# First feed-forward of a two-layer transformer block: a down product in plain float32 or as three products of high and low parts

## The chip, the cores and the metric

The kernel runs on one core of a Trainium2 chip. The metric is the device time in microseconds (us) of one execution. The core's engines are TensorE (PE, matrix products into PSUM), VectorE (DVE), ScalarE (ACT), GpSimd (POOL) and SyncE (SP, which issues DMAs). Each runs its own list of instructions in order; semaphores order them against each other.

## The reference

1024 tokens of 256 features pass through attention, a feed-forward, a second attention and a second feed-forward, each with a layer norm ahead and a residual add behind. The change is in the first feed-forward:

```
h = silu(x @ w_gate) * (x @ w_up)          # x: (4, 256, 256), w_gate, w_up: (256, 1024)
g = h.reshape(B, S, I // 4, 4)             # of every four hidden values keep
_, idx = top_k(abs(g), 2)                  # the two that are largest by magnitude
h_sparse = (g * mask(idx)).reshape(B, S, I)
out = h_sparse @ w_down                    # w_down: (1024, 256)
x = x + out
```

## The kernel before, in words

Hidden values lie transposed: hidden features on the 128 partitions, tokens along the free dimension. The feed-forward is cut in four quarters k = 0 to 3. Quarter k holds tokens of half k // 2 (512 tokens) and hidden features of half k % 2 (512 features, as four columns j of 128). The features are laid out so that the four columns of a quarter are the four members of each group, so the 2-of-4 choice compares whole columns. With i = 4k + j the columns are numbered 0 to 15.

**Gate and up** (`pe_gate_up`, line 1000). For each column i, 12 products on TensorE: gate and up, two halves of the contraction, and for each three products of high and low parts. This is the kernel's way to near-float32 accuracy at the rate of the rounded type fp32r: a value is split into a high part (rounded to fp32r) and a low part (value minus high), and high x high, high x low and low x high are added up in PSUM. They use PSUM banks 0 to 5, so column i waits for silu and hidden product of column i - 3.

**Activation, product, choice.** ScalarE makes silu(gate) (`act_silu`, line 1157) and VectorE multiplies it with up into the hidden buffer (`dve_hidden`, line 1266). ScalarE takes magnitudes (`act_abs`, line 1217). VectorE compares them, three ops of 1024 columns a quarter with both inputs in SBUF (`dve_compare`, line 1358), counts in 16-bit arithmetic (`dve_count`, lines 1366 to 1372) and keeps or clears the values in place, two ops of 1024 columns (`dve_keep`, line 1379), which raise the semaphore `hs`.

**Down** (`pe_down`, line 1074 for the first feed-forward, line 1078 for the second; `pe_last_down0`, line 1094, for the first one's last quarter). For each of four token tiles of a quarter TensorE adds up the four columns' products with w_down into PSUM bank 6 or 7; VectorE adds the result to x (`dve_xadd`, line 1342). In the first feed-forward the operands are plain float32: hidden buffer and raw weights. Each such product is two records in the profile. In the second, three products of parts are used, with high parts from ScalarE (line 1202) and low parts from VectorE (line 1457) in the buffers `encf`, and weights split by GpSimd in `b_w`.

**Order.** It is written out by hand. TensorE (`pe_ffn0`): columns 0 to 10, down quarter 0, columns 11 to 13, down quarter 1, columns 14 and 15, four transposes of the next layer norm, down quarter 2; quarter 3 follows in the head of the second attention. VectorE (`dve_ffn0`) does for each k two compares, a hidden product, the third compare, the first count step, a hidden product, the votes, a hidden product, then residual adds, keeps, and the last hidden product. ScalarE (`act_ffn0`) has silu and magnitudes in turn: in the round of k it is silu 4k+4, 4k+5, 4k+6, magnitudes 4k+4 and 4k+5, silu 4k+7, magnitudes 4k+6 and 4k+7. GpSimd ends the first attention with `pool_drain0` (row statistics, low parts of some weights; `ln_pool`, line 325) and then waits for the layer norm of the second attention. The down weights are loaded by SP long before, into `raw_b`. In the second attention GpSimd splits weights (`split`, lines 888 and 890) and forms sums of W2 (line 1575).

Of the kernel before, what the change touches and what calls it, by code (L numbers as in the profile page):

```python
# [22 lines left out]
F32 = mybir.dt.float32  # L23
# [3 lines left out]
ALU = mybir.AluOpType  # L27
# [9 lines left out]
UNITS = 8 * PAIRS  # L37
# [69 lines left out]
def build(nc, x_in, wa, wax, wb, wdown0, w2t, consts, scales, shuffle, out):  # L107
    with ExitStack() as ctx:
        def sb(name, shape, dt=F32):
            return ctx.enter_context(nc.sbuf_tensor(name, shape, dt))  # L110

        def sem(name):
            return ctx.enter_context(nc.semaphore(name))
# [11 lines left out]
        b_w = [[sb(f"b_{part}{s}", [P, WB_FFN], F32R) for part in ("hi", "lo")] for s in range(2)]  # L125
# [4 lines left out]
        with ExitStack() as whole:  # L130
            def sb1(name, shape):
                return whole.enter_context(nc.sbuf_tensor(name, shape, F32))
# [3 lines left out]
            raw_b = sb1("raw_b", [P, 2, WB_FFN])  # L136
# [75 lines left out]
        encf = [e[:, :, :].rearrange("p h t -> p (h t)").rearrange("p (j t) -> p j t", j=4) for e in enc]  # L212
# [34 lines left out]
        at = [{n: sem(f"L{L}_{n}") for n in names} for L in range(2)]  # L247
        raw_as = [[sem(f"L{L}_raw_a{s}") for s in range(2)] for L in range(2)]
        raw_bs = [[sem(f"L{L}_raw_b{s}") for s in range(2)] for L in range(2)]
        fnames = ("whi", "w", "gate", "up", "silu", "h", "abs", "cmp", "hs", "hi", "lo", "whi2", "w2", "down", "xadd")  # L250
        ff = [{n: sem(f"F{f}_{n}") for n in fnames} for f in range(2)]
        s_late, s_late_hi, s_late_lo = (sem("late_columns_" + n) for n in ("loaded", "high", "low"))
        s_bf, s_hadmm, s_hadev = (sem(n) for n in ("butterfly", "had_product", "w2_made"))
        s_blank, s_had = sem("blank_set"), sem("hadamard_loaded")
# [24 lines left out]
        def need_pieces(eng, f, last):  # L279

            n = pieces_until(f, last)
            if f == 0 and n > POOL_PIECES:
                eng.wait_ge(ff[0]["w2"], n - POOL_PIECES)
            else:
                eng.wait_ge(ff[f]["w"], n)
# [55 lines left out]
        def ln_act(act, st, t, bk):  # L342
            i = 8 * st + t
            act.wait_ge(ln["turned"], i + 1)
            src = bank[bk][:, 0:D].rearrange("p (c t) -> p c t", c=NC)
            nc.scalar.copy(xT[0][:, :, t * P:(t + 1) * P], src).then_inc(ln["hi"], 1)
# [539 lines left out]
        def split(hi, lo, src, eng, s_hi, wait, s_lo):  # L886

            nc.gpsimd.tensor_tensor(hi, src, zero[:, 0:1].broadcast_to(list(src.shape)), ALU.add).then_inc(s_hi, 1)  # L888
            wait()
            nc.gpsimd.tensor_tensor(lo, src, hi.bitcast(F32), ALU.subtract).then_inc(s_lo, 1)  # L890
# [158 lines left out]
        def hidden(f, k, j):  # L1049

            return hid_late[k - 2][:, j, :] if f == 0 and k >= 2 else hid[:, k % 2, j, :]

        def pe_down(pe, f, k, tiles=range(4)):
            s, L = ff[f], at[f]
            t = k % 2
            for tt in tiles:
                d = 4 * k + tt
                if tt == 0:
                    if f == 0:
                        pe.wait_ge(s["hs"], 4 * k + 4)  # L1060
                        if k < 2:
                            pe.wait_ge(raw_bs[0][t], 16 * 5)
                    else:
                        pe.wait_ge(s["hi"], 4 * k + 4)
                        pe.wait_ge(s["lo"], 4 * k + 4)
                        if k < 2:
                            need_pieces(pe, f, f"b{t}")
                if d < 2:
                    pe.wait_ge(ln["lo"], 16 * f + 16)
                if d >= 2:  # L1070
                    pe.wait_ge(s["xadd"], d - 1)
                if f == 0:
                    for j in range(4):
                        mm = pe.matmul(bank[6 + d % 2][:, 0:D], hidden(0, k, j)[:, tt * P:(tt + 1) * P],  # L1074
                                       raw_b[:, t, j * D:(j + 1) * D], start=j == 0, stop=j == 3)
                else:
                    for q, (j, (l, r)) in enumerate([(j, p) for j in range(4) for p in PASSES]):
                        mm = pe.matmul(bank[6 + d % 2][:, 0:D], encf[l][:, j, tt * P:(tt + 1) * P],  # L1078
                                       b_w[t][r][:, j * D:(j + 1) * D], start=q == 0, stop=q == 11)
                mm.then_inc(s["down"], 1)  # L1080
# [71 lines left out]
        def act_silu(act, f, i):  # L1152
            s = ff[f]
            act.wait_ge(s["gate"], i + 1)
            if i >= 2:
                act.wait_ge(s["h"], i - 1)
            nc.scalar.activation(gate[:, i % 2, :], bank[2 * (i % 3)][:, :], ACT.Silu).then_inc(s["silu"], 1)  # L1157
# [46 lines left out]
        def act_hadamard(act, q):  # L1204
            act.wait_ge(s_hadmm, q + 1)
            nc.scalar.mul(w2_a[:, 2 * q:2 * q + 2, :].rearrange("p a d -> p (a d)"), bank[S_BANK + q % 2][:, :],
                          float(HID) ** -0.5).then_inc(s_hadev, 1)

        def act_abs(act, i):

            k, j = i // 4, i % 4
            act.wait_ge(ff[0]["h"], i + 1)
            if i == 0:
                act.wait_ge(at[0]["pv"], UNITS)
            elif k and j == 0:
                act.wait_ge(ff[0]["cmp"], 3 * k)
            nc.scalar.activation(mag[:, j, :], hidden(0, k, j), ACT.Abs).then_inc(ff[0]["abs"], 1)

        def act_ffn0(act):
            for i in range(4):  # L1220
                act_abs(act, i)
            for k in range(3):
                i = 4 * (k + 1)
                act_silu(act, 0, i)
                if k == 0:
                    ln_act(act, 1, 7, 7)
                act_silu(act, 0, i + 1)
                act_silu(act, 0, i + 2)
                act_abs(act, i)
                act_abs(act, i + 1)  # L1230
                if k == 2:
                    act_next_a(act)
                act_silu(act, 0, i + 3)
                act_abs(act, i + 2)
                act_abs(act, i + 3)
            for t in range(4):
                ln_act(act, 2, t, LN2_BANK[t])
# [157 lines left out]
        def act_next_a(act):  # L1395

            act.wait_ge(raw_as[1][0], 16 * A_PARTS[1])
            act.wait_ge(ff[0]["up"], 12)
            for part in range(4):
                cs = slice(part * A0, (part + 1) * A0)  # L1400
                nc.scalar.copy(a_w[0][0][:, cs], raw_a[:, 0, cs]).then_inc(at[1]["a0hi"], 1)
# [141 lines left out]
        def pool_drain0(pool):  # L1543

            for t in range(1, 8):
                if t < 4:
                    pool.wait_ge(ln["xn"], 8 + t)
                    pool_late_lo(pool, t)
                elif t in (5, 6):
                    pool.wait_ge(ln["xn"], 8 + t)  # L1550
                    pool_piece_lo(pool, 0, t - 5)
                ln_pool(pool, 1, t)
# [134 lines left out]
        @block.gpsimd  # L1687
        def _(pool):
            nc.gpsimd.memset(zero[:, :], 0.0).then_inc(s_zero, 1)
            nc.gpsimd.memset(neg_half[:, :], -0.5).then_inc(s_half, 1)  # L1690
            nc.gpsimd.memset(rms_eps[:, :], RMS_EPS).then_inc(s_half, 1)
            pool.wait_ge(s_zero, 1)
            pool.wait_ge(s_half, 2)
            for t in range(2):
                ln_pool(pool, 0, t)
            pool.wait_ge(s_rope, 16)
            pool.wait_ge(s_scl, 16)
            for a in (2, 0):
                if a == 0:
                    pool.wait_ge(s_scq, 1)  # L1700
                nc.gpsimd.tensor_tensor(cos_t[:, :, a, :], cos_c, scl[:, a // 2, :].unsqueeze(1).broadcast_to([P, 2, DH]),
                                        ALU.mult).then_inc(s_cos, 1)
            ln_pool_two(pool, 0, 2)
            pool_b(pool, 0, None, 0, 0)
            slots(pool, 0, pool_slot, pool_head0, pool_tail(pool, 0))
            pool_drain0(pool)
            for t in range(4):
                ln_pool(pool, 2, t)
            slots(pool, 1, pool_slot, pool_head, pool_tail(pool, 1))
            for n in range(2, 5):  # L1710
                pool_piece_lo(pool, 1, n)
            for n in range(5, len(pieces[1])):
                if pieces[1][n][0] == "b1" and pieces[1][n - 1][0] == "b0":
                    pool.wait_ge(ff[1]["lo"], 4)
                pool_piece(pool, 1, n)
# [4 lines left out]
        def _(act):  # L1720
# [8 lines left out]
            for L in range(2):  # L1729
# [35 lines left out]
                if L == 0:  # L1765
                    act_drain0(act)
                (act_ffn0, act_ffn1)[L](act)

        @block.vector
# [216 lines left out]
```

## Time and profile before

| | |
|---|---|
| median of 3 runs | 673.9 us (673.75 to 675.7) |
| profiled execution | 675.06 us |
| its span | 673.3 us |
| granted TensorE clock, mean | 0.997 |
| busy: PE, DVE, ACT, POOL | 98%, 83%, 66%, 53% of the span |

Busy is the share of the span in which an engine had at least one instruction at work. Products overlap in the pipe and their ends are modelled, so a product's duration (0.28 us for 256 columns) is more than the distance between two starts. Times of rows are us from the span's start.

### The profile page before, as it was taken

To read this page: it belongs to the slowest core of one execution; us is meant where nothing else is said; L and a number is where in the kernel's file an instruction comes from. 1 tells how busy PE (TensorE), PEld (TensorE's weight loads), DVE (VectorE), ACT (ScalarE), POOL (GpSimd) and SP (SyncE) were. 2 spreads that over 40 slices of the span, in tenths; PEclk is the share of its full clock that TensorE was granted. 3 is DMA by queue.
4 is the path that set the end of the run, shared out by engine and by line. 5 is a ranking of instruction groups with operands and counts; after the bars stand their busy time and mean duration, and the time that the engine had idled before them with its cause. 6 is when DMAs were issued, how large, how long until landed. Compare 5 with 4: busy or idle time off the path is not lost.

```text
span 673.3 us, 15093 instructions
## 1 busy us (share of the span) xinstructions
PE 659.8 (98%) x4153; PEld 588.3 (87%) x4153; DVE 556.0 (83%) x1705; ACT 446.8 (66%) x1721; POOL 360.1 (53%) x557
## 2 busy tenths in 40 slices
PE   8899999999999998999999999999999999999998
PEld 4689999999999997888879999999999999978887
DVE  7889999899989878969866998989999898795443
ACT  3899999999999875422347676666676666763222
POOL 5899999999999944002068961523232324028000
PEclk8999999999999999999999999999999999999999
DMA  7156666765656640100035656566556656000000
GB/s 243 38 129 137 136 144 156 169 135 133 141 125 139 130 173 0 48 1 1 16 107 121 155 124 152 116 142 135 135 132 130 142 125 139 17 1 1 1 31 32
DMA packets 242594, 69.55 MB, mean 103 GB/s; under 512 B 184400, under 2 KB 238544, under 8 KB 242384
## 3 DMA queue, kind: packets, MB, share of 16 engines
q1 hardware_dynamic: 219280, 56.53, 38.1%
q10 hardware_dynamic: 23232, 12.06, 6.0%
q8 instruction: 35, 0.57, 0.4%
q14 instruction: 47, 0.39, 0.2%
HBM read 45.29 MB, written 23.27 MB: 102 GB/s over the span
## 4 chain that ended last, share of the span: by engine, by line
PE 89%; DVE 6%; issue 2%; POOL 1%; ACT 1%; DVEq 0%; POOLq 0%; ACTq 0%
PE bank L543 13%; PE bank L427 12%; PE bank L1000 12%; PE bank L535 11%; PE bank L564 7%; PE bank L395 6%; PE bank L470 4%; PE bank L388 4%; PE bank L472 4%; PE bank L487 3%; PE bank L1074 3%; PE bank L465 3%; PE bank L1078 3%; DVE x L743 1%; PE bank L1094 1%
## 5 line engine op out<-in xcount | busy, mean ns | idle before, releaser
L713 ACT ACTIVATE probs<-scores,negmax 128x128 f32<-128x128 f32 (+1 forms) x256 | 117.1, 470 | 6.1 <-DVE negmax L798 4.9
L621 ACT CAST enc_hi<-bank 128x256 fp32r<-128x256 f32 x128 | 48.8, 381 | 66.0 <-PE bank L472 62.6
L888 POOL TENSOR_TENSOR a_hi<-raw_a,zero 128x384 fp32r<-128x384 f32 (+1 forms) x60 | 44.2, 736 | 71.1 <-PE bank L564 71.1
L325 POOL TENSOR_TENSOR ln_r<-ln_ve,neg_half 128x1 f32<-128x1 f32 x26 | 17.0, 654 | 118.3 <-DVE ln_ve L299 118.3
L427 PE MATMUL bank<-b_hi,enc_hi 128*128 128x256 f32 x256 | 77.8, 304 | 0.5 <-DVE x L743 0.5
L774 DVE STREAM_TRANSPOSE blocks<-probs 128x384 f32<-128x384 f32 x113 | 64.8, 574 | 11.7 <-ACT probs L713 9.9
L427 PE MATMUL bank<-b_hi,enc_lo 128*128 128x256 f32 x256 | 72.1, 282 | 0.0
L427 PE MATMUL bank<-b_lo,enc_hi 128*128 128x256 f32 x256 | 71.8, 281 | 0.0
L743 DVE SCALAR_TENSOR_TENSOR x<-bank,rinv,x 128x256 f32<-128x256 f32 x144 | 67.4, 468 | 2.2 <-PE bank L427 0.9
L754 DVE TENSOR_TENSOR enc_lo<-bank,enc_hi 128x256 fp32r<-128x256 f32 x128 | 53.4, 417 | 16.5 <-PE bank L395 9.4
L906 POOL TENSOR_TENSOR rot_a<-rot_a,rot_b 128x384 f32<-128x384 f32 x64 | 64.9, 1014 | 0.2 <-DVE rot_b L875 0.2
L904 POOL TENSOR_TENSOR rms_r<-meansq,neg_half 128x3 f32<-128x3 f32 x64 | 54.8, 856 | 6.6 <-DVE meansq L873 2.3
L1157 ACT ACTIVATE gate<-bank 128x512 f32<-128x512 f32 x32 | 19.1, 598 | 58.7 <-PE bank L1000 57.9
L890 POOL TENSOR_TENSOR a_lo<-raw_a,a_hi 128x384 fp32r<-128x384 f32 (+1 forms) x60 | 53.8, 896 | 4.7
L535 PE MATMUL bank<-a_hi,xT_hi 128*128 128x512 f32 x128 | 51.9, 408 | 2.7 <-DVE xT_lo L352 1.7
L713 ACT ACTIVATION_READ_ACCUMULATOR probs<-scores,negmax 128x1 f32 x256 | 53.4, 209 | 0.0
L543 PE MATMUL bank<-xT_hi,a_hi 128*128 128x512 f32 x128 | 52.0, 406 | 0.3 <-DVE xT_lo L352 0.3
L661 ACT ACTIVATE gate<-bank 128x128 f32<-128x128 f32 x192 | 50.6, 282 | 1.8 <-PE bank L535 1.8
L427 PEld LDWEIGHTS bank<-b_hi,enc_hi 128*128 128x128 f32 x256 | 48.5, 189 | 3.4 <-issue 0.9
L543 PE MATMUL bank<-xT_lo,a_hi 128*128 128x512 f32 x128 | 50.5, 395 | 0.0
L427 PEld LDWEIGHTS bank<-b_lo,enc_hi 128*128 128x128 f32 x256 | 48.5, 190 | 2.3
L543 PE MATMUL bank<-xT_hi,a_lo 128*128 128x512 f32 x128 | 50.3, 393 | 0.0
(186 smaller groups left out, 2330.6 us busy)
## 6 DMA issues: line engine op xcount, KB each, us to landing
arrived<-shuffle SPq DMA_DIRECT2D x452, 48.0 KB, 2.2
shuffle<-blocks ACTq DMA_DIRECT2D x57, 192.0 KB, 2.5
shuffle<-blocks SPq DMA_DIRECT2D x56, 192.0 KB, 2.5
raw_a<-in_wa SPq DMA_DIRECT2D x40, 192.0 KB, 3.2
raw_b<-in_wb SPq DMA_DIRECT2D x16, 256.0 KB, 3.0
raw_a<-in_wa SPq DMA_DIRECT2D x32, 128.0 KB, 2.7
hid_last<-in_wax SPq DMA_DIRECT2D x2, 512.0 KB, 3.8
w_a<-in_w2t SPq DMA_DIRECT2D x1, 1024.0 KB, 5.3
```

What stands on the lines that cost most here:

```text
L427: mm = pe.matmul(output_bank(L, m)[:, cols], enc[l][:, h, t * P:(t + 1) * P], b_w[slot][r][:, h * D:(h + 1) * D], start=i == 0 and not (on ...
L535: mm = pe.matmul(ps[:, :], xT[l][:, g, t * P:(t + 1) * P], a_w[slot][r][:, g * 512:(g + 1) * 512], start=i == 0, stop=i == 5)
L543: mm = pe.matmul(ps[:, :], a_w[slot][l][:, g * 768 + w * P:g * 768 + (w + 1) * P], xT[r][:, g, half * 512:(half + 1) * 512], start=i == 0, ...
L661: nc.scalar.activation(gate[:, m % 2, a * DH:(a + 1) * DH], bank[PJ_BANK + m % 2][:, a * DH:(a + 1) * DH], ACT.Square, scale=float(DH) ** ...
L713: nc.scalar.activation(probs[:, c % 4, c0:c1], scores[:, c % 2, c0:c1], ACT.Exp, bias=negmax[:, c % 2, r:r + 1], scale=-1.0, accum_out=row ...
L743: nc.vector.scalar_tensor_tensor(out=x[:, m % 8, :], in0=output_bank(L, m)[:, hh * D:(hh + 1) * D], scalar=rinv[:, u, r:r + 1], in1=x[:, m ...
L754: nc.vector.tensor_tensor(enc[1][:, w % 2, dst], bank[O_BANK][:, 0:D], enc[0][:, w % 2, dst].bitcast(F32), ALU.subtract).then_inc(s["elo"], 1)
L774: nc.vector.transpose(blocks[:, c % 2, :], probs[:, c % 4, :]).then_inc(s_blocks[L], 1)
L890: nc.gpsimd.tensor_tensor(lo, src, hi.bitcast(F32), ALU.subtract).then_inc(s_lo, 1)
L904: nc.gpsimd.tensor_tensor(rms_r[:, t, :], meansq[:, m % 2, :], neg_half[:, 0:3], ALU.pow).then_inc(s["rp"], 1)
L906: nc.gpsimd.tensor_tensor(rot_a[:, m % 2, :], rot_a[:, m % 2, :], rot_b[:, m % 2, :], ALU.add).then_inc(s["radd"], 1)
L1000: mm = pe.matmul(ps[:, :], a_w[t][l][:, c0:c0 + P], xT[rr][:, g, th * 512:(th + 1) * 512], start=q == 0, stop=q == 5)
```

## The change

In quarters 0 and 1 of the first feed-forward the down product becomes three products of parts, as in the second feed-forward; quarters 2 and 3 stay plain. ScalarE copies the kept hidden values into high parts (`act_hi0`), GpSimd subtracts to get low parts (`pool_lo0`), and GpSimd splits the down weights of both halves into `b_w` (`pool_down_weights`, through `split`: an add of zero for the high, a subtraction for the low part, 512 columns at a time, two pairs for each half).

```diff
             for tt in tiles:
                 d = 4 * k + tt
                 if tt == 0:
-                    if f == 0:
+                    if f == 0 and k < 2:
+                        pe.wait_ge(s["hi"], 4 * k + 4)
+                        pe.wait_ge(s["lo"], 4 * k + 4)
+                        pe.wait_ge(s_down_lo, 2 * (t + 1))
+                    elif f == 0:
                         pe.wait_ge(s["hs"], 4 * k + 4)
-                        if k < 2:
-                            pe.wait_ge(raw_bs[0][t], 16 * 5)
                     else:
...
-                if f == 0:
+                if f == 0 and k >= 2:
                     for j in range(4):
                         mm = pe.matmul(bank[6 + d % 2][:, 0:D], hidden(0, k, j)[:, tt * P:(tt + 1) * P],
                                        raw_b[:, t, j * D:(j + 1) * D], start=j == 0, stop=j == 3)
...
+        def act_hi0(act, k, half):
+
+            if k == 0:
+                act.wait_ge(at[0]["op"], UNITS)
+            else:
+                act.wait_ge(ff[0]["down"], 4 * k)
+            act.wait_ge(ff[0]["hs"], 4 * k + 2 * half + 2)
+            for j in (2 * half, 2 * half + 1):
+                nc.scalar.copy(encf[0][:, j, :], hidden(0, k, j)).then_inc(ff[0]["hi"], 1)
+
+        def pool_lo0(pool, k):
+
+            for j in range(4):
+                pool.wait_ge(ff[0]["hi"], 4 * k + j + 1)
+                nc.gpsimd.tensor_tensor(encf[1][:, j, :], hidden(0, k, j), encf[0][:, j, :].bitcast(F32),
+                                        ALU.subtract).then_inc(ff[0]["lo"], 1)
+
+        def pool_down_weights(pool, t):
+
+            pool.wait_ge(raw_bs[0][t], 16 * 5)
+            pool.wait_ge(at[0]["op"], UNITS)
+            for n in range(2):
+                cs = slice(512 * n, 512 * (n + 1))
+                split(b_w[t][0][:, cs], b_w[t][1][:, cs], raw_b[:, t, cs], pool, s_down_hi,
+                      lambda: pool.wait_ge(s_down_hi, 2 * t + n + 1), s_down_lo)
...
                 act_silu(act, 0, i)
                 if k == 0:
                     ln_act(act, 1, 7, 7)
+                elif k == 1:
+                    act_hi0(act, 0, 0)
+                    act_hi0(act, 0, 1)
+                else:
+                    act_hi0(act, 1, 1)
                 act_silu(act, 0, i + 1)
                 act_silu(act, 0, i + 2)
                 act_abs(act, i)
...
                 act_silu(act, 0, i + 3)
                 act_abs(act, i + 2)
+                if k == 1:
+                    act_hi0(act, 1, 0)
                 act_abs(act, i + 3)
...
             pool_drain0(pool)
+            for t in range(2):
+                pool_down_weights(pool, t)
+            for k in range(2):
+                pool_lo0(pool, k)
             for t in range(4):
                 ln_pool(pool, 2, t)
```

## Rows read from the trace of the kernel before

**Rows 1.** The page's part 4: the chain's shares by engine.
```profile
PE 89%; DVE 6%; issue 2%; POOL 1%; ACT 1%; DVEq 0%; POOLq 0%; ACTq 0%
```
**Rows 2.** The chain in order of time, first feed-forward: start, us, what.
```profile
277.05 16.35 PE bank L1000 x72
293.40 6.91 PE bank L1074 x32
300.31 8.17 PE bank L1000 x36
308.48 6.91 PE bank L1074 x32
```
**Rows 3.** Timeline of PE, second feed-forward: start us, us, engine, line, op, names.
```profile
619.80 0.28 PE L1078 MATMUL bank<-b_hi,enc_hi 128*128 128x256 f32 x1
...
625.56 0.40 PE L1000 MATMUL bank<-xT_hi,a_hi 128*128 128x512 f32 x1
```
**Rows 4.** Timeline of POOL, weights of 128x512 in the second feed-forward.
```profile
611.43 1.29 POOL L890 TENSOR_TENSOR b_lo<-w_a,b_hi 128x512 fp32r<-128x512 f32 x1
612.68 1.04 POOL L888 TENSOR_TENSOR b_hi<-w_a,zero 128x512 fp32r<-128x512 f32 x1
613.80 1.30 POOL L890 TENSOR_TENSOR b_lo<-w_a,b_hi 128x512 fp32r<-128x512 f32 x1
```
**Rows 5.** Timeline of POOL in the first feed-forward.
```profile
271.62 0.94 POOL L325 TENSOR_TENSOR ln_r<-ln_ve,neg_half 128x1 f32<-128x1 f32 x1 [2.77 <-DVE ln_ve L299]
311.62 0.55 POOL L325 TENSOR_TENSOR ln_r<-ln_ve,neg_half 128x1 f32<-128x1 f32 x1 [39.06 <-DVE ln_ve L299]
313.34 1.48 POOL L325 TENSOR_TENSOR ln_r<-ln_ve,neg_half 128x1 f32<-128x1 f32 x1 [1.18 <-DVE ln_ve L299]
```
**Rows 6.** Timeline of DVE in the first feed-forward.
```profile
276.07 2.37 DVE L1358 TENSOR_TENSOR work<-v 128x1024 uint8<-128x1024 f32 x2 [0.55 <-ACT v L1217]
...
280.74 0.42 DVE L1367 TENSOR_TENSOR work<-work 128x512 uint16<-128x512 uint16 x1
...
281.42 0.68 DVE L1266 TENSOR_TENSOR qk<-bank,gate 128x512 f32<-128x512 f32 x1
...
300.69 2.35 DVE L1379 SCALAR_TENSOR_TENSOR qk<-work,qk 128x1024 f32<-128x1024 uint8 x2
...
313.19 1.23 DVE L1379 SCALAR_TENSOR_TENSOR v<-work,v 128x1024 f32<-128x1024 uint8 x1
```
**Rows 7.** Timeline of ACT ahead of the first down quarter.
```profile
286.27 0.63 ACT L1217 ACTIVATE v<-qk 128x512 f32<-128x512 f32 x1 [1.24 <-DVE qk L1266]
286.81 0.58 ACT L1157 ACTIVATE gate<-bank 128x512 f32<-128x512 f32 x1
```
**Rows 8.** Timeline of DVE, a scale op of the last layer norm.
```profile
606.60 1.37 DVE L332 TENSOR_SCALAR xn<-x,ln_mv,ln_r 128x256 f32<-128x256 f32 x1 [0.66 <-POOL ln_r L325]
```
**Rows 9.** Timeline of POOL, same stretch.
```profile
606.53 3.83 POOL L1511 TENSOR_TENSOR a_lo<-raw_a,a_hi 128x512 fp32r<-128x512 f32 x3
```
**Rows 10.** Timeline of DVE, second attention.
```profile
375.63 1.39 DVE L762 TENSOR_TENSOR turned<-arrived,turned 128x256 fp32r<-128x256 f32 x1
...
380.05 0.42 DVE L762 TENSOR_TENSOR turned<-arrived,turned 128x256 fp32r<-128x256 f32 x1
```
**Rows 11.** Timeline of POOL, same stretch.
```profile
374.32 2.41 POOL L1575 TENSOR_TENSOR work<-w_a 128x1024 f32<-128x1024 f32 x1
376.69 1.23 POOL L888 TENSOR_TENSOR a_hi<-hid_last,zero 128x512 fp32r<-128x512 f32 x1
```
**Rows 12.** Windows of PE near the start: stretch, us, busy, granted clock, DMA.
```profile
14.00:16.00 2.00, 2.00 (x6) 0.50 1.01 351
16.00:17.00 1.00, 1.00 (x6) 0.56 0.70 248
```
**Rows 13.** Timeline of PE just ahead of it.
```profile
11.81 0.97 PE L339 MATMUL bank<-cst,xn 128*128 128x128 f32 x4 [0.97 <-DVE xn L332]
13.67 0.79 PE L535 MATMUL bank<-a_hi,xT_hi 128*128 128x512 f32 x1 [0.89 <-DVE xT_lo L352]
```

More of the change, by code:

```diff
@@ L251, in build @@
         ff = [{n: sem(f"F{f}_{n}") for n in fnames} for f in range(2)]
+        s_down_hi, s_down_lo = sem("F0_down_weights_high"), sem("F0_down_weights_low")
         s_late, s_late_hi, s_late_lo = (sem("late_columns_" + n) for n in ("loaded", "high", "low"))
```

## The prediction

> **What bounds the kernel now.** I read the chain of waits first, then the tensor engine's records in order of time around the two products, then the vector engine's, ScalarE's and GpSimd's in the same stretch, and last the places where a GpSimd and a vector instruction overlap. The chain is PE for 89% of the span [rows 1]. From 277 to 315 us, where the change lies, it is PE alone: 72 products of the gate/up stage (line 1000) in 16.35 us, 0.227 us each, then the first down quarter, 32 records in 6.91 us, three gate/up columns in 8.17, the second down quarter in 6.91 [rows 2]. PE never waits here, so time taken out of PE is gained, and a wait put before the down product is paid in full. GpSimd is idle here for 39.06 us [rows 5]. VectorE is not: from 276 to 292 its ops touch one another (compare, count, hidden product, keep) [rows 6].
>
> I write h5 for the hidden product of column i=5 (line 1266), C for a compare of 1024 columns (line 1358), K for a keep (line 1379).
>
> **Part 1, the products.** A quarter is 4 token tiles by 4 columns: 16 plain products, two records each, 6.91 us [rows 2]. After the change it is 48 products of 256 columns. The second feed-forward has just these: from the first at 619.80 to the gate/up product behind them at 625.56, 48 in 5.76 us, 0.120 each [rows 3]. Gain 1.15 us a quarter, 2.3 us for both, all on the path. Quarters three and four stay as they are.
>
> **Part 2, GpSimd's weights.** Four pairs of 128x512, high then low. The same shapes take 1.04 and 1.29 us; from start to start a high costs 1.12, a low 1.25 [rows 4], so 4 x 2.37 = 9.5 us. They start when GpSimd's last row statistic of the drain ends, 271.62 + 0.94 = 272.56 [rows 5], and alone would be done at 282.0, long before PE wants them at 293.4.
>
> **Part 3, high parts on ScalarE.** A 128x512 pass from SBUF to SBUF takes 0.63, pitch 0.54 [rows 7]. For quarter one they stand behind silu 8 at 286.81 [rows 7]: all four done at about 287.4 + 3 x 0.55 + 0.62 = 289.6. Two of quarter two stand behind the keeps that start at 300.69 [rows 6], two behind silu 12. ScalarE idles before both; by themselves these copies cost nothing.
>
> **Part 4, low parts on GpSimd.** Four at 1.25 us, the first at about 288.0: done at 293.1, just when PE arrives. Quarter two: first at 303.4, last done at about 308.5, where PE, 1.15 us earlier than before, arrives at 307.2; but the keeps too come 1.15 earlier, because they stand behind the four residual adds of quarter one. Wait 0 to 0.2. If nothing disturbed anything the sum is -2.3 + 0.2 = -2.1 us.
>
> **Part 5, what GpSimd's work does to VectorE, and back.** This decides. The trace has overlaps of both kinds:
> - VectorE comes second: the scale op (256 columns, one SBUF input) starts at 606.60 inside the first of three 1.28 us GpSimd ops that began at 606.53 [rows 9] and takes 1.37 [rows 8]; it ends 0.15 after that first op does. A 256-column subtraction of two SBUF operands starts at 375.63, takes 1.39 instead of the 0.42 of the one at 380.05 [rows 10], and ends at 377.02, 0.29 after the GpSimd op that ran till 376.73 [rows 11]. 0.29 is its pure streaming time; it had been held to the end of the other's instruction.
> - GpSimd comes second: its next 128x512 high part (376.69) takes 1.23 instead of 1.04 and ends 0.90 after the vector op [rows 11]. A tiny power op takes 1.48 instead of 0.55 when it starts just behind a keep: 313.34 + 1.48 = 314.82 [rows 5], 0.40 after the keep's end at 313.19 + 1.23 = 314.42 [rows 6].
>
> So a vector op with two SBUF inputs (or a fast one-input op) and a GpSimd op exclude each other for a whole instruction, and the waiting one goes next; I count a C or K as +1.10 after GpSimd's end, a 256-cycle op +0.28, a GpSimd high +0.90, a low +1.16 after VectorE's end. Ops that read PSUM (hidden product, residual add) are not held.
>
> The walk, quarter one. GpSimd: high at 272.56, low held a little by the scale op, to 275.2, high to 276.2. C at 276.07 is held: 277.3. Then they alternate: low 278.4, C 279.5, high 280.4, C (after h4 and a PSUM op) 281.5, low 282.7, count op 282.85, high 283.75, count op 284.0, low 285.2 (weights done), count op 285.5. h5 starts at 285.4 instead of 281.42 [rows 6] and ends 286.1. PE needs h5 for column 8, which it would start at 277.05 + 3 x 2.73 = 285.2 less the record's 0.16: stall 1.1 us. Behind it: votes, h6, two keeps to 289.7, h7 to 290.2, and only then abs 7, which ScalarE has in front of silu 8: silu 8 at 290.8 instead of 286.81, high parts from 291.4 to 293.7. The low parts meet the next round of compares: C to 292.5, low 293.7, C 294.8, low 295.9, count op, low 297.2, count op, low 298.7. PE starts quarter one at 298.8; it was ready at 294.4: stall 4.4 us. Queued behind PE's wait is all its later work, since the order is fixed.
>
> Quarter two: PE's column 11 starts 5.5 - 1.15 = 4.4 later than before, and with it the residual adds and keeps (300.69 becomes 305.1). High parts 307.2 to 308.4, GpSimd's first low to 309.2, then C 310.3, low 311.5, C 312.6, low 313.7, C 314.8, low 316.0. PE was ready at 312.7: stall 3.4 us. VectorE then follows PE at +6.6 to +6.9, and nothing between there and the second attention gives it back: PE is 98% busy by the page and next stages follow its order.
>
> Sum: 1.1 + 4.4 + 3.4 - 2.3 = +6.6 us.
>
> The weak place is the 16-bit count ops (one takes 0.42 us [rows 6]): no row shows one of them in an overlap. If only the float compares and keeps were held, h5 would be done at 283.1, in time for PE; quarter one would start at about 296.2 (stall 3.0), quarter two would wait 3.3, and the sum would be +4.0. I take +6.6, since a fast op with even fewer SBUF inputs was held [rows 8].
>
> **Part 6, the clock.** Before, PE drops from 2.4 to 1.2 GHz once after the start-up: two waits of 0.97 and 0.89 us close together [rows 13], then 0.50 is granted from 14 to 16 and 0.56 on the mean in 16 to 17 [rows 12]. With PE starting at 13.67 that is some 3 us at half speed, less what of it falls on the hand-over at the start: 1.3 us of work lost. Stalls of 4.4 and 3.4 us are longer than the pair, so I add 1.3 us twice; the lower bound is 0, the upper 2 each (the low stretch could last longer than there). Taken: +2.6.
>
> **Forecast.** +6.6 + 2.6 = +9.2 us. The profiled execution took 675.06 us, 1.76 around its span of 673.3; it becomes 684.3, and the median, 1.2 lower at 673.9, becomes 683.1 us.
>
> **Rivals.**
> A. Exclusion as above, but the clock holds at one or both stalls: +6.6 to +7.9, 680.5 to 681.8 us. For it: the stalls are single, and the one drop in the trace came early. Against: they are much longer than the waits of that drop.
> B. Only part of the exclusion (the count ops free, or one engine keeps winning so that the other's work is merely put off): +4.0, with clock up to +6.6: 677.9 to 680.5 us. Against it: waiters of both kinds got in after one instruction [rows 8 to 11].
> C. The other side: the four low parts come in 1.25 us steps and the weights are done at 282, so nothing is held and the two quarters just get shorter: -2.1, 671.8 us. It decides at 293.2: if the fourth low part of quarter one is done by then the change gains; each 1.15 us of lateness eats one quarter's gain. For it: GpSimd's idle 39 us and the even pitch in rows 4. Against it: those rows were free of two-input vector ops, while here compares stand in the same microseconds.
> D. The delays balance the gain: within 0.3% (2 us, about what a measurement of this kernel can tell from no change). Needs total stalls of 0.3 to 4.3 us.
>
> That the change does not do what it says is no rival: 48 products at 0.120 are in the second feed-forward's records.
>
> **Chances.** Forecast 0.45, A 0.22, B 0.17, C 0.10, D 0.06. Faster 0.11 (C and a bit of D), same 0.05, slower 0.84. The range has to take A and B and clock stretches longer than the one seen (+2 each instead of 1.3, and a tie lost in the walk, 1.2): 676 to 686.5 us; it leaves out C.
>
> **What would show it.** In the profile after: VectorE's compares with means near 2 us instead of 1.22, GpSimd's low parts near 1.6 to 2.3; h5 about 4 us later; PE idle before the first product of quarter one about 4.4 us and of quarter two about 3.4, released by GpSimd's low part; a granted clock of 0.5 in the microseconds behind both; the 48 products at 0.120 elsewhere. Compares still at 1.22 and PE without idle would prove me wrong, and so would an h5 on time with low parts late, which would mean that GpSimd alone yields.

## The result and the profile after

The changed kernel takes 684.15 us (median of 4, 683.33 to 684.32) against 673.93 for the kernel before (673.75 to 675.7): ratio 1.0146, 95% interval 1.0132 to 1.016, slower by 10.2 us. The forecast was 683.1. The profiled execution took 684.22 us, its span is 682.4, the mean granted clock 0.992 instead of 0.997. Rows of the changed kernel carry its own line numbers.

The chain of waits of the changed kernel, in order of time through the first feed-forward (start, us, what; line 1001 is the gate/up product, 1081 the three products, 1302 the hidden product):

```profile
284.43 0.61 DVE qk L1302
285.04 0.14 issue
285.18 8.40 PE bank L1001 x36
293.58 3.99 issue
297.58 7.47 PE bank L1081 x48
305.05 8.19 PE bank L1001 x36
313.23 2.99 issue
316.22 8.60 PE bank L1081 x48
324.82 5.47 PE bank L1001 x24
```

Before, this stretch of the chain was TensorE alone [rows 2]. Now it comes to TensorE from VectorE's h5 at 284.43, and there are two stretches called "issue" ahead of the down products: TensorE waits for the low parts. Its waits in this part of the kernel, by the view of waits (total, times, longest):

```profile
PE bank L1081 <- issue: 7.0, 2, 4.0
PE bank L1001 <- DVE qk L1302: 1.0, 1, 1.0
```

So the stalls are 1.0 at column 8, 4.0 ahead of quarter 0 and 3.0 ahead of quarter 1. The quarters themselves take 7.47 and 8.60 us, not 5.76. Windows of TensorE over both (stretch, us, busy and count, granted clock, DMA share, GB/s) say why:

```profile
298.00:300.00 2.00, 2.00 (x13) 0.56 0.00 0
300.00:302.00 2.00, 2.00 (x12) 0.58 0.00 0
302.00:304.00 2.00, 2.00 (x19) 1.00 0.00 0
...
314.00:316.00 2.00, 0.00 (x0) 0.83 0.00 0
...
320.00:322.00 2.00, 2.00 (x11) 0.50 0.00 0
322.00:324.00 2.00, 2.00 (x18) 0.96 0.00 0
```

For a time the clock is 1.2 instead of 2.4 GHz. By windows of 0.5 us it is low from about 298.3 us, 0.7 behind the end of the first long wait, to 301.7, and again from about 315.2, while TensorE still waits for the second, to 322.1. Sum: 1.0 + 4.0 + 3.0 for the stalls, 7.47 + 8.60 - 2 x 6.91 = 2.25 for the quarters, together 10.25 us, which is what the medians differ by. (The 36 products behind the stall at column 8 take 8.40 us where later columns take 8.19; with these 0.2 the sum is 10.5, as in the two profiles over this stretch, below.)

GpSimd in the changed kernel (timeline; line 889 makes a high, 891 a low part of the weights, 1226 the low parts of the hidden values):

```profile
271.46 1.12 POOL L889 TENSOR_TENSOR b_hi<-raw_b,zero 128x512 fp32r<-128x512 f32 x1
...
275.17 2.21 POOL L891 TENSOR_TENSOR b_lo<-raw_b,b_hi 128x512 fp32r<-128x512 f32 x1
277.33 2.02 POOL L889 TENSOR_TENSOR b_hi<-raw_b,zero 128x512 fp32r<-128x512 f32 x1
279.43 2.24 POOL L891 TENSOR_TENSOR b_lo<-raw_b,b_hi 128x512 fp32r<-128x512 f32 x1
281.64 1.08 POOL L889 TENSOR_TENSOR b_hi<-raw_b,zero 128x512 fp32r<-128x512 f32 x1
282.80 1.35 POOL L891 TENSOR_TENSOR b_lo<-raw_b,b_hi 128x512 fp32r<-128x512 f32 x1
290.91 6.57 POOL L1226 TENSOR_TENSOR enc_lo<-qk,enc_hi 128x512 fp32r<-128x512 f32 x4 [6.76 <-ACT enc_hi L1220]
308.17 7.95 POOL L1226 TENSOR_TENSOR enc_lo<-qk,enc_hi 128x512 fp32r<-128x512 f32 x4 [10.70 <-ACT enc_hi L1220]
```

And VectorE beside it, to be read against [rows 6] (line 1394 is a compare, 1402 to 1404 are count ops):

```profile
274.99 3.46 DVE L1394 TENSOR_TENSOR work<-v 128x1024 uint8<-128x1024 f32 x2 [0.55 <-ACT v L1246]
...
279.31 1.21 DVE L1394 TENSOR_TENSOR work<-v 128x1024 uint8<-128x1024 f32 x1
280.55 1.27 DVE L1402 TENSOR_SCALAR work<-work 128x512 uint16<-128x512 uint16 x1
281.74 1.26 DVE L1403 TENSOR_TENSOR work<-work 128x512 uint16<-128x512 uint16 x1
282.92 1.51 DVE L1404 TENSOR_TENSOR work<-work 128x512 uint16<-128x512 uint16 x1
284.36 0.68 DVE L1302 TENSOR_TENSOR qk<-bank,gate 128x512 f32<-128x512 f32 x1
...
308.51 4.28 DVE L1394 TENSOR_TENSOR work<-v 128x1024 uint8<-128x1024 f32 x2
```

The two engines take turns. The count op at 280.55 ends at 281.82, 0.15 after GpSimd's op (279.43 + 2.24 = 281.67); the next ends at 283.00, 0.28 after the next GpSimd op (282.72); the third at 284.43, again 0.28 after (284.15). Where VectorE goes first GpSimd pays: its 1.04 and 1.29 become 2.02 and 2.24. Two compares take 3.46 and 4.28 instead of 2.37. Note how little the page's totals tell: VectorE is still busy 83% of the span, GpSimd 57%.

### The profile page after: what moved, and what is told of

The parts are those of the page before. It is cut to its first block, busy times and chain, and to the rows that moved or that the text cites. A ratio compares the mean times of both kernels' runs of the same rounds, so it can differ in the third digit from the quotient of the medians.

```text
span 682.4 us, 15189 instructions
## 1 busy us (share of the span) xinstructions
PE 660.5 (97%) x4185; PEld 589.6 (86%) x4185; DVE 567.1 (83%) x1705; ACT 449.4 (66%) x1729; POOL 386.6 (57%) x573
## 4 chain that ended last, share of the span: by engine, by line
PE 85%; DVE 7%; issue 3%; ACT 2%; POOL 1%; DMA 1%; SPq 0%; DVEq 0%; POOLq 0%; ACTq 0%
PE bank L544 13%; PE bank L428 12%; PE bank L536 11%; PE bank L1001 10%; PE bank L565 7%; PE bank L396 6%; PE bank L1081 5%; PE bank L471 4%; PE bank L389 4%; PE bank L473 4%; PE bank L466 3%; PE bank L488 3%; DVE x L744 1%; PE bank L1077 1%; PE bank L1097 1%
## 5 line engine op out<-in xcount | busy, mean ns | idle before, releaser
L622 ACT CAST enc_hi<-bank 128x256 fp32r<-128x256 f32 x128 | 48.8, 381 | 72.3 <-PE bank L473 70.3
L536 PE MATMUL bank<-a_hi,xT_hi 128*128 128x512 f32 x128 | 51.4, 404 | 2.6 <-DVE rot_b L876 1.3
L889 POOL TENSOR_TENSOR b_hi<-raw_b,zero 128x128 fp32r<-128x128 f32 (+1 forms) x68 | 32.1, 472 | 36.8 <-PE bank L428 36.8
```

The lines of the kernel that those rows point to most:

```text
L536: mm = pe.matmul(ps[:, :], xT[l][:, g, t * P:(t + 1) * P], a_w[slot][r][:, g * 512:(g + 1) * 512], start=i == 0, stop=i == 5)
```

## Experiments

The profiles reach this stretch at times up to 2.1 us apart (GpSimd's last row statistic of the drain starts between 270.34 and 272.44). One reason is the drop of the clock near 14 us [rows 12]: it is in some executions of a kernel and not in others, and not in the profile of the changed kernel. The executions of the kernel before that stood beside the last three experiments have a median of 675.35 us where the mean granted clock is 0.997, as in the profile with the drop, and of 674.03 where it is 0.999 or 1.000. So I also give a local length for each profile: from the start of GpSimd's last row statistic of the drain (271.62 in [rows 5]) to the first plain product of quarter 2. Before: 271.62 to 321.56, 49.94 us. Changed kernel: 270.54 to 331.00, 60.46, that is +10.5. "The kernel before" had a median of 674.7 us beside the first four and 674.9 beside the last three. The rows of an experiment carry the line numbers of its own kernel; each is named where it is not plain.

**1. The parts are made, and nobody waits for them.**

```diff
-                    if f == 0 and k < 2:
-                        pe.wait_ge(s["hi"], 4 * k + 4)
-                        pe.wait_ge(s["lo"], 4 * k + 4)
-                        pe.wait_ge(s_down_lo, 2 * (t + 1))
-                    elif f == 0:
+                    if f == 0:
                         pe.wait_ge(s["hs"], 4 * k + 4)
...
-                if f == 0 and k >= 2:
+                if f == 0:
...
             else:
                 act.wait_ge(ff[0]["down"], 4 * k)
+                act.wait_ge(ff[0]["lo"], 4)
```

The last wait keeps ScalarE from writing over high parts that GpSimd has not read.

> ScalarE and GpSimd make all parts as in the changed kernel, but TensorE takes the plain products again and waits for the kept values only, as before the change (the parts are waited for ahead of quarter 2). If exclusion between GpSimd and VectorE is at work, VectorE is held although nobody waits for the parts: column 8 still stalls 1.0 us, and the residual adds come late behind the held compares and counts, which TensorE meets at the third token tile of quarters 0 and 1: 676 to 681 us. Rival, that only TensorE's wait for the low parts costs and VectorE's delay is harmless: 675 us or less.

Measured: 682.39 us (679.84 to 684.8), ratio 1.0115 (1.0077 to 1.0153); local length 59.6, +9.7. The waits of TensorE in this part (line 1079 the plain products, 1381 the residual add, 1305 the hidden product):

```profile
PE bank L1079 <- DVE x L1381: 4.9, 2, 3.0
PE bank L1001 <- DVE qk L1305: 1.0, 1, 1.0
```

The column 8 stall is the same, and the two others now come at the third token tile of each quarter, released by the residual add. The clock falls too (0.51 granted from 300 to 305 us), so the second half of quarter 0, 16 records, takes 6.64 us instead of about 3.5. The rival (only the wait for low parts costs) fell.

The four executions are of two kinds. The profiled one and 684.80 have a mean granted clock of 0.992 and 0.993. The other two, 679.84 and 680.40, have 0.999 and 1.000, so neither a drop here nor one near 14 us; they lie inside the range I gave, which had no lost clock in it. Against the 673.91 us that the kernel before takes beside them without a drop, these two lost 5.9 and 6.5 us. So VectorE's delay by itself costs about 6 us through stalls, and in two of four executions some 3 us more through the clock.

**2. No work on GpSimd.**

```diff
-                        pe.wait_ge(s["lo"], 4 * k + 4)
-                        pe.wait_ge(s_down_lo, 2 * (t + 1))
...
-            for t in range(2):
-                pool_down_weights(pool, t)
-            for k in range(2):
-                pool_lo0(pool, k)
```

> The three products stay, with ScalarE's high parts; GpSimd makes neither low parts nor weights. The low operand is replaced by the high one and the weights by what the attention left in the buffer, so the output is not the reference's. Exclusion theory: with GpSimd silent VectorE is not held, no stall, no drop of the clock, and the two quarters are 1.15 us shorter each: 671.6 to 672.0 us. Rival, that ScalarE's copies or the products themselves cost in this place: 673.9 us or more.

Measured: 671.96 us, ratio 0.9963 (0.9949 to 0.9977); local length 47.7, -2.3. The chain (line 1082 the three products):

```profile
276.97 16.39 PE bank L1001 x72
293.35 5.75 PE bank L1082 x48
...
307.29 5.75 PE bank L1082 x48
```

The products bring what they were to bring, 1.16 us a quarter, ScalarE's copies cost nothing, and nothing waits. Everything that is lost comes from GpSimd's part: its work and the waits for it.

**3. No weights, but the low parts.**

```diff
-                        pe.wait_ge(s_down_lo, 2 * (t + 1))
...
-            for t in range(2):
-                pool_down_weights(pool, t)
```

> GpSimd makes the low parts but does not split the weights (the products use what the attention left there, so the output is not the reference's). Exclusion theory: the stall at column 8 (1.0 us) goes, silu 8 is on time, the low parts of quarter 0 still meet two compares and the counts and end about 1.5 us after TensorE is ready, which should cost no clock; quarter 1 is as in the changed kernel (3.0 us of stall, 2.8 of clock, 1.15 gained): 678 to 680 us. Rival, that the weights are the whole trouble and the low parts alone keep pace: 672 us.

Measured: 678.37 us, ratio 1.005 (1.0031 to 1.0068); local length 53.9, +4.0. In the chain, line 1083 is the three products:

```profile
293.93 1.28 issue
295.21 5.99 PE bank L1083 x48
...
309.39 2.99 issue
312.38 7.49 PE bank L1083 x48
```

The stalls are as worked out: none at column 8, 1.28 us ahead of quarter 0 with the clock kept, 2.99 ahead of quarter 1. The clock is lost there, but costs 1.5 us, not the 2.8 that I had put in; behind a wait of the same 2.99 us the changed kernel lost 2.6. The low parts of four columns take 6.63 us on GpSimd even with VectorE on time. So of the 10.5 us the weights bring 6.5: 1.2 at column 8, 2.7 of longer stall ahead of quarter 0 (silu 8 and with it the high parts are late), and 2.6 of clock in the two quarters. The low parts cost 4.0, net of the gain.

**4. Products in the waits.** Twelve products that nobody reads, between the waits for single low parts:

```diff
+                        if d < 2:
+                            pe.wait_ge(ln["lo"], 16)
+                        else:
+                            pe.wait_ge(s["xadd"], d - 1)
+                        for n in range(1, 4):
+                            pe.wait_ge(s["lo"], 4 * k + n)
+                            for _ in range(4):
+                                pe.matmul(bank[6][:, :], a_w[1][0][:, 0:P], xT[0][:, 0, 512:1024], start=True, stop=True)
```

> The changed kernel with 12 products of 512 columns that nobody reads put between the waits for the single low parts, ahead of quarters 0 and 1. If the 4.5 us by which the two quarters take longer than 5.76 us each come from the halved clock, they go and the stalls stay: 679.3 to 680.3 us, granted clock 1.00 throughout. Rival, that the quarters are slow because operands or residual adds come late: 684 us or more.

Measured: 681.16 us (679.82 to 684.27), ratio 1.0104 (1.0073 to 1.0135); local length 56.5, +6.5, which is 4.0 less than the changed kernel. In the chain, line 1089 is the three products and 1068 the twelve that nobody reads:

```profile
299.52 5.99 PE bank L1089 x48
...
313.70 2.72 PE bank L1068 x12
316.42 0.32 issue
316.74 5.99 PE bank L1089 x48
```

Both quarters take 5.99, the granted clock is 1.00 throughout, and both still wait for the last low part. The clock's share is 4.0 of the 10.5 us; from the chains it is 7.47 + 8.60 - 2 x 5.99 = 4.1. The median is 0.9 above the range I gave, though two of the four executions (679.82 and 680.21) lie in it. The profiled one is the longest, 684.27 us; its local length explains 6.5 of this, and what made it longer elsewhere was not traced.

**5. Fills in place of additions.** Each GpSimd operation becomes three fills of the same tile:

```diff
-                nc.gpsimd.tensor_tensor(encf[1][:, j, :], hidden(0, k, j), encf[0][:, j, :].bitcast(F32),
-                                        ALU.subtract).then_inc(ff[0]["lo"], 1)
+                pool_fill(pool, encf[1][:, j, :], ff[0]["lo"])
```

`pool_fill` issues `nc.gpsimd.memset` of zeros on the tile three times, each waiting for the one before.

> The changed kernel, but each GpSimd addition or subtraction is replaced by three fills with zeros of the same 128x512 tile (so the low parts and weights are zeros and the output is not the reference's). GpSimd then writes SBUF and reads nothing. If what excludes the two engines is the reading side, compares and counts keep 1.22 and 0.42 us beside the fills, TensorE does not stall and the time is that of the kernel without GpSimd's work, 672 us, as long as a tile's fills take under 1.5 us. If any GpSimd access to SBUF excludes VectorE, compares stretch and the time is 676 us or more.

Measured: 675.71 us, ratio 1.0017 (1.0004 to 1.003); local length 51.4, +1.4. The fills of a tile took 1.65 us, more than the 1.5 I had allowed, and TensorE waits 1.47 and 1.75 us for the last of them. The median is close to the 676 us of the other theory, so the trace has to decide. VectorE beside GpSimd's fills, which follow one another from 271.2 to 284.7 us (line 1403 the compare, 1411 and 1412 the first two count ops):

```profile
274.80 2.36 DVE L1403 TENSOR_TENSOR work<-v 128x1024 uint8<-128x1024 f32 x2 [0.55 <-ACT v L1255]
278.01 1.22 DVE L1403 TENSOR_TENSOR work<-v 128x1024 uint8<-128x1024 f32 x1
279.26 0.51 DVE L1411 TENSOR_SCALAR work<-work 128x512 uint16<-128x512 uint16 x1
279.69 0.41 DVE L1412 TENSOR_TENSOR work<-work 128x512 uint16<-128x512 uint16 x1
```

Compares and two-input count ops are not held at all; the one-input count op is (0.51 instead of 0.29). What the two-input ops compete for is the reading side. The Trainium skill, "SBUF — State Buffer", section "Who interferes with whom", says the same: a two-input VectorE op contends only with a GpSimd op that reads SBUF. The trace agrees: the compares keep 1.22 us.

**6. Low parts on VectorE, weights still on GpSimd.**

```diff
-            for k in range(2):
-                pool_lo0(pool, k)
...
                 dve_compare(dve, k, 2)
+                if k >= 1:
+                    dve_lo0(dve, k - 1)
                 dve_count(dve, k, 0)
```

> The low parts of both quarters are subtracted by VectorE (0.69 us each, pitch 0.60, behind the third compare), GpSimd splits only the weights as in the changed kernel. Exclusion theory: the 1.0 us stall at column 8 stays, since the weights meet the same compares; quarter 0 starts 1 to 1.5 us late because silu 8 is late, quarter 1 about 2 us late, since VectorE is full there; no wait is over 2 us, so the clock holds: 675 to 677.5 us. Rival, that giving VectorE 4.8 us more work is no better than the exclusion: 682 us or more.

Measured: 680.21 us (678.32 to 682.83), ratio 1.0076 (1.0052 to 1.0101); local length 55.0, +5.1. Neither theory's number: 680.2 lies between. The waits are 1.0 at column 8 and 1.87 ahead of quarter 1, as expected, and 2.06 ahead of quarter 0, above the 1 to 1.5 expected. And the clock did not hold (the chain, then two windows of TensorE; line 1081 is the three products):

```profile
294.09 2.06 issue
296.14 6.17 PE bank L1081 x48
...
310.50 1.87 issue
312.37 7.49 PE bank L1081 x48
```

```profile
296.00:302.00 6.00, 5.86 (x47) 1.00 0.00 0
...
314.00:316.00 2.00, 2.00 (x11) 0.50 0.04 8
```

Against the 5.99 us of a quarter that starts out of a wait with its clock kept (experiments 3 to 5), quarter 0 lost 0.2 and quarter 1 lost 1.5 us, though the second wait is the shorter one, and a wait of 1.75 us in experiment 5 cost none. The 0.2 is not the clock's, which is granted in full from 296 to 302 us: the third token tile starts at 299.17, just behind a residual add that VectorE, late by the low parts, ends at 299.12. Better than the changed kernel by 4 us all the same, with 4.8 us more work on the fuller engine.

**7. One quarter, its weights early, its low parts on VectorE.** Quarter 1 is plain again. 512 columns of weights are split at 247 us, in the end of the attention, and 512 behind the drain:

```diff
                 if f == 0 and t == -1:
                     pool_late_lo(pool, 0)
+                    pool.wait_ge(at[0]["op"], UNITS - 8)
+                    pool_down_weights(pool, 0, (0,))
...
             pool_drain0(pool)
-            for t in range(2):
-                pool_down_weights(pool, t)
-            for k in range(2):
-                pool_lo0(pool, k)
+            pool_down_weights(pool, 0, (1,))
...
                 dve_compare(dve, k, 2)
+                if k == 1:
+                    dve_lo0(dve, k - 1)
                 dve_count(dve, k, 0)
```

> Only quarter 0 takes three products; its low parts are made by VectorE behind the third compare; GpSimd splits only the first half's weights, 512 columns at about 248 us in the end of the attention and 512 right behind the drain, both before VectorE's first compare. Quarter 1 is plain. Exclusion theory: nothing is held on the path, the low parts are there by 292.7, and one quarter is 1.15 us shorter: 672.6 to 673.1 us against 673.9 to 674.7 for the kernel before (ratio 0.998 to 0.9985). Rival, that VectorE's 2.4 us more of work ahead of the residual adds eats it: 673.9 us or more.

Measured: 672.41 us (671.82 to 673.12, 6 runs), ratio 0.996 (0.9946 to 0.9974). It is the fastest of the kernels that make every part, faster than both kernels compared here, and its median is 0.2 below the range I gave. Local length 48.8, -1.13, just the one quarter's gain (line 1083 the three products, 1079 the plain ones):

```profile
275.94 16.35 PE bank L1001 x72
292.29 5.75 PE bank L1083 x48
...
306.23 6.91 PE bank L1079 x32
```

The median is 2.5 us below that of the kernel before beside it, but part of this is the clock near 14 us: all six executions here have a mean granted clock of 1.000, while 9 of the 17 of the kernel before have 0.997. Against the 674.03 us of the others the gain is 1.6 us, of which the quarter explains 1.13; the rest was not traced to a cause. The experiment changes three things at once (one quarter less, the weights moved, the low parts on VectorE) and does not say what each is worth.

## Why the prediction was right

- **The products** (-1.15 a quarter): right, 5.75 us in experiments 2 and 7.
- **Weights on GpSimd** hold VectorE: right by place and nearly by time. h5 starts 284.36 - 270.54 = 13.8 us behind GpSimd's last statistic instead of 9.8, 4.0 late as forecast; the stall is 1.0, not 1.1. The walk had weights done at 285.2, that is 13.6 behind that statistic; they were done at 284.15, also 13.6 behind.
- **The count ops**, the weak place: held, 1.27, 1.26 and 1.51 us instead of 0.29 and 0.42. Rival B, which had them free, is out. The Trainium skill, "SBUF — State Buffer", section "Who interferes with whom", names no type for a two-input op that contends; the trace agrees, with the 1.26 and 1.51 us of the two-input 16-bit ops.
- **Stalls ahead of the quarters**: forecast 4.4 and 3.4, measured 4.0 and 3.0. The step is right, and the turns that the two engines take are those of the walk. Counted from GpSimd's last statistic, the products of quarter 0 start after 27.04 us (forecast 27.18) and TensorE is ready for them after 23.04 (forecast 22.78), of which 0.2 is the slower start behind the stall at column 8. In quarter 1 the last low part ends 11.07 us behind the end of quarter 0 instead of 11.44.
- **What the wait is for.** The text put the price on TensorE's wait for the low parts. Experiment 1 shows that this was too narrow: without that wait the residual adds behind the same held ops stop TensorE, 4.9 us in two waits. In the profiled execution +9.7 of +10.5 stay, in the two executions without a drop of the clock about 6, near the 6.5 that the changed kernel loses with its waits filled. The price hangs on VectorE's queue and the low parts alike.
- **The clock**: forecast 1.3 twice. The term was mis-sized. The quarters took 7.47 and 8.60 where 5.99 is the time out of a wait at full clock: 1.5 and 2.6 lost, together 4.1; filling the waits gave back 4.0. The 1.3 for one such drop was sound: it is what the kernel before loses by it (675.35 against 674.03). But behind the second stall TensorE ran at 1.2 GHz for some 6 us, where the drop of before had lasted 3.
- **The sum**: 0.9 us too much stall, 1.5 too little clock, and 0.7 for three starts out of a wait that I had not counted make +10.5 out of the +9.2 forecast, over this stretch; the medians show +10.2. That the forecast is within 1.1 us is in part luck, since the first two errors point opposite ways.
- Two figures beside the forecast do not come out of their own terms. Rival B has quarter one start at 296.2 with a stall of 3.0, but TensorE was ready at 293.4, which makes 2.8. And the upper bound of 686.5 is higher than its terms give, 673.9 + 6.6 + 4 + 1.2 = 685.7.

## What to carry to other kernels

GpSimd's idle time is not free if VectorE is full at that moment with ops that read two SBUF operands: here each pair of such ops was done one after the other, and both engines came late. Before moving a tensor-tensor op to GpSimd, look for overlaps of that kind elsewhere in the trace and lay the new ops beside VectorE's list; place them where VectorE mostly reads PSUM, as experiment 7 did. And allow for the clock behind a stall of TensorE: here it cost between nothing and 0.9 of the stall (2.6 us behind 3.0).

## What the runs showed that I had not expected

The length of a wait alone does not tell whether the clock falls, nor for how long. Waits of 1.28, 1.47, 1.75 and 2.06 us cost no clock, one of 1.87 cost 1.5 (experiments 3, 5 and 6), and two of 2.99 cost 1.5 (experiment 3) and 2.6 (changed kernel). The two short waits of [rows 13], from which the prediction read its drop, stand in the profile of the changed kernel too:

```profile
13.63 0.50 PE L536 MATMUL bank<-a_hi,xT_hi 128*128 128x512 f32 x1 [0.89 <-DVE xT_lo L353]
```

The product behind them takes 0.50 us, not 0.79, and the granted clock is 1.00 there. What else decides stays open; no run was made for it.

A fill of 128x512 float32 takes GpSimd about 0.55 us, three of them 1.65, more than one addition of a broadcast zero (1.04).
